# Masked 16-wide cross attention: scores as one float32r pass over four 32-row blocks, transposes two heads behind, values three

## The chip, the cores and the metric

The kernel runs on one core of a Trainium2 chip. The metric is the device time of one execution in microseconds (us), lower is better. TensorE (PE) does the matmuls, VectorE (DVE), ScalarE (ACT) and GpSimd (POOL) the rest; SyncE (SP) issues the DMAs of this stage.

## The reference, cut to what matters

Four layers of cross attention and feed-forward on x of 16 batches x 112 rows x 256, with a context of 16 x 375 x 256. The change touches the first layer's attention alone: 16 heads of width 16, a mask from a running sum, biases.

```
q = (queries @ wq.T + bq).reshape(b, s, h, dh)
k = (patch_representations @ wk.T + bk).reshape(b, p, h, dh)
v = (patch_representations @ wv.T + bv).reshape(b, p, h, dh)
scores = jnp.einsum('bqhd,bkhd->bhqk', q, k) * scale
mask = jnp.arange(p)[None, None, :] > patch_idx[:, :, None]
scores = jnp.where(mask[:, None, :, :], jnp.finfo(scores.dtype).min, scores)
attn = jax.nn.softmax(scores, axis=-1)
out = jnp.einsum('bhqk,bkhd->bqhd', attn, v).reshape(b, s, d)
return out @ wo.T + bo
```

## The kernel before

One function, `cross_attention`, writes three of the four attention stages. With heads of 64 (`wide`) it takes another branch; the first stage is the branch `not wide`. All data are float32. The stage loops over 16 batches and in each over 16 heads, written out as a program for every engine; counters (semaphores) tie them.

For head h TensorE does, in this order: `scores(h)`, a bf16 matmul that adds the mask (identity by `barred`, L451) and a float32 matmul of the head's queries with the keys (L453; the trace has two records for each); `turn(h-1)`, three transposes of the previous head's probabilities (L464); `values(h-2)`, three float32 matmuls (L494, six records). `lag` is the distance of the transposes. The queries lie in `q`, where the 128 rows of a half of the model hold only the head's 16 rows and zeros elsewhere (`headmask`), so the matmul contracts 128 rows of `kT` of which 16 count.

VectorE takes the maximum of a head's scores from PSUM (`head_max`, L752) and copies the transposed probabilities to SBUF (`take_probsT`, L758). ScalarE does the exponential (L608). The scores alternate between two PSUM banks, and the transposes between two.

The projections of the next batch and the output of the last one are cut into pieces, set by hand in the table `order`: behind which head TensorE does K0, K1 (keys, L398), L0, L1 (transposes of the normalised rows), Q0 (queries), V0 to V2 (values), O0 and Y0 (output). They use a ring of two banks, and `slots` says which piece had the bank before. Before the first head of a batch TensorE waits for that batch's Q and K to be taken from PSUM. `first` does the pieces of batch 0 ahead of the heads. SP loads the contexts two batches ahead (L328).

The stages with heads of 64 already split their keys and queries into high and low parts of type float32r (`keys_hi`, `keys_lo`, `q_hh`, `q_ll`) and use three matmuls a head for the scores (L437, L439, L441).

Of the kernel before, what the change touches and what calls it, by code (L numbers as in the profile page):

```python
# [6 lines left out]
F32 = mybir.dt.float32  # L7
# [116 lines left out]
def cross_attention(nc, core, name, ctx_in, w, dh, mask=None):  # L124
# [25 lines left out]
    else:  # L150
        order = {0: ["K0"], 2: ["K1"], 5: ["O0"], 7: ["Y0", "L0", "L1"], 9: ["Q0"], 10: ["V0"],
# [5 lines left out]
    lag = 3 if wide else 1  # L157
    NB = 4 if wide else 2
# [3 lines left out]
    with ctx:  # L162
# [23 lines left out]
        else:  # L186
# [4 lines left out]
            q = [sb(f"q{i}", [P, H, T]) for i in range(2)]  # L191
            kT = [sb(f"kT{i}", [P, EC, S]) for i in range(2)]
# [17 lines left out]
        if mask:  # L210
# [4 lines left out]
            keys = sb("keys", [T, S])  # L215
            headmask = sb("headmask", [P, P // dh])
            barred = [sb(f"barred{i}", [T, S], BF16) for i in range(2)]
# [17 lines left out]
        nweights = 4 + (4 if biased else 0) + (4 if mask else 0)  # L235
# [75 lines left out]
        with nc.Block() as block:  # L311

            @block.sync
            def _(sp):
# [6 lines left out]
                if mask:  # L321
                    sp.dma_start(steps[:, :], mask["steps"]).then_inc(weights.sem, 16)
                    sp.dma_start(upto[:, :], mask["upto"]).then_inc(weights.sem, 16)
                    sp.dma_start(keys[:, :], mask["keys"].partition_broadcast(T)).then_inc(weights.sem, 16)
                    sp.dma_start(headmask[:, :], mask["headmask"]).then_inc(weights.sem, 16)
# [5 lines left out]
                if wide:  # L331
# [13 lines left out]
                    return  # L345
                load(Batch(0, 0))
                load(Batch(0, 1))
                with sp.Fori(0, (B - 2) // 2) as i:
                    for k in (2, 3):
                        b = Batch(i, k)  # L350

                        sp.wait_ge(made["V"].sem, made["V"].at(count("V%d" % (NV - 1), b + -2)))
                        load(b)
# [4 lines left out]
            def _(pe):  # L358
# [67 lines left out]
                def scores(b, h):  # L426
# [29 lines left out]
                def turn(b, h):  # L456
# [4 lines left out]
                    else:  # L461
                        pe.wait_ge(exped.sem, exped.at(H * b.n + h + 1))
                    for j in range(J):
# [20 lines left out]
                def values(b, h):  # L484
# [8 lines left out]
                    for j in range(J):  # L493
                        ins = pe.matmul(bank[0:T, h % G * dh:(h % G + 1) * dh], probsT[h % 2][:, j, :],  # L494
# [3 lines left out]
                def heads(b, b_first, b_last, split_next=True):  # L498
                    where = slots(b_first)
                    for h in range(H):  # L500
# [5 lines left out]
                        if not wide and not (b_first and h < 2):  # L506
# [1952 lines left out]
```

## Time and profile before

| what | value |
|---|---|
| median of three runs | 4162.86 us (4162.65 to 4162.91) |
| time of the profiled execution | 4161.14 us |
| its span, first to last instruction | 4159.3 us |
| TensorE busy | 3536.1 us (85%) |
| VectorE, ScalarE, GpSimd busy | 1574.0, 1536.9, 1197.4 us |
| first score matmul to the last of the stage | 52.6 to 613.7 us |

The time is the span and 1.8 us around it. The masked stage is some 560 of the 4159 us, and the change touches nothing behind it. The profile's slices show TensorE at 9 tenths or more in all of this stage.

### The profile page before, as it was taken

What the parts mean: (1) busy time and instruction counts of PE and PEld (TensorE: products, weight loads), DVE (VectorE), ACT (ScalarE), POOL (GpSimd) and SP (SyncE); (2) the same over time, 40 slices, a digit from 0 to 9 for tenths busy, and PEclk for the clock granted to TensorE, in tenths of its full rate; (3) what the DMA queues carried; (4) which work ended last, traced back from release to release, by engine and by line L of the source; (5) the groups of instructions that cost most, each with busy time, mean ns of one, the idle gap of its engine ahead of it and who ended that gap; (6) DMA issues with size and microseconds to landing.
All of it is one profiled execution on the core that took longest, in us unless ns stands there. A gap on an engine that the chain in (4) does not pass through costs nothing. (4 is left out here: it accounts for less than half of the span.)

```text
span 4159.3 us, 67079 instructions
## 1 busy us (share of the span) xinstructions
PE 3536.1 (85%) x22014; PEld 2897.3 (70%) x22014; DVE 1574.0 (38%) x3464; ACT 1536.9 (37%) x4297; POOL 1197.4 (29%) x1312
## 2 busy tenths in 40 slices
PE   5999992996897873975999999759599999997999
PEld 4777772885565652654889888658488888885665
DVE  3555552001225541014444544300344444444444
ACT  2333330432224550212555555324255444551111
POOL 0000003002000002014666666410466656661000
PEclk9999995998898976987999999779799999997999
DMA  3000002886110003331000000077200000000001
GB/s 117 12 11 11 11 1 82 304 309 211 51 34 4 0 2 106 116 112 34 9 7 9 9 7 5 3 241 280 74 10 9 9 9 9 8 1 12 23 19 33
DMA packets 102019, 240.30 MB, mean 58 GB/s; under 512 B 24682, under 2 KB 73644, under 8 KB 84012
## 3 DMA queue, kind: packets, MB, share of 16 engines
q1 hardware_dynamic: 94188, 219.82, 16.1%
q0 software_dynamic: 7680, 18.36, 1.7%
q8 instruction: 108, 1.77, 0.2%
q14 instruction: 43, 0.35, 0.0%
HBM read 208.78 MB, written 29.36 MB: 57 GB/s over the span
## 5 line engine op out<-in xcount | busy, mean ns | idle before, releaser
L642 POOL TENSOR_SCALAR L_probs<-L_probs,L_inverse 112x375 f32<-112x375 f32 x512 | 645.2, 1260 | 86.9 <-issue 86.9
L752 DVE TENSOR_REDUCE L_negmax<-bank 112x1 f32<-112x375 f32 x768 | 417.5, 544 | 559.7 <-PE bank L441 344.6
L608 ACT ACTIVATE L_probs<-bank,L_negmax 112x375 f32<-112x375 f32 x768 | 439.4, 572 | 407.1 <-DVE L_negmax L752 407.1
L464 PEld LDWEIGHTS bank<-ident,L_probs 112*125 112x125 f32 x2304 | 360.4, 189 | 108.3 <-ACT L_probs L608 47.1
L640 POOL TENSOR_TENSOR L_inverse<-L_sums,neg_one 112x1 f32<-112x1 f32 x512 | 315.2, 616 | 349.7 <-ACT L_probs L608 344.1
L464 PE MATMUL bank<-ident,L_probs 112*125 112x112 f32 x2304 | 376.0, 271 | 22.0 <-issue 10.3
L596 ACT ACTIVATE L_probsT<-bank 125x336 f32<-125x336 f32 x512 | 231.3, 452 | 315.4 <-PE bank L464 313.3
L479 PE MATMUL bank<-L_probsT,v 125*64 125x112 f32 x3072 | 206.1, 270 | 1.1 <-ACT L_probsT L596 1.1
L453 PE MATMUL bank<-L_kT,L_q 128*112 128x375 f32 x512 | 203.5, 478 | 0.0
L437 PE MATMUL bank<-L_keys_hi,L_q_hh 128*112 128x376 f32 x512 | 184.3, 360 | 8.9 <-DVE L_keys_lo L695 6.5
L581 ACT ACTIVATE v<-bank 125x512 f32<-125x512 f32 x192 | 114.9, 598 | 197.3 <-PE bank L391 197.3
L494 PE MATMUL bank<-L_v,L_probsT 125*112 125x16 f32 x1536 | 172.4, 238 | 0.1
L441 PE MATMUL bank<-L_keys_hi,L_q_ll 128*112 128x376 f32 x512 | 171.8, 336 | 0.0
L494 PEld LDWEIGHTS bank<-L_v,L_probsT 125*112 125x112 f32 x1536 | 171.4, 178 | 0.2 <-DVE L_probsT L758 0.2
L439 PE MATMUL bank<-L_keys_lo,L_q_hh 128*112 128x376 f32 x512 | 171.5, 335 | 0.0
L479 PEld LDWEIGHTS bank<-L_probsT,v 125*64 125x64 f32 x3072 | 150.6, 137 | 29.3 <-ACT L_probsT L596 1.6
L1396 ACT ACTIVATE L0t_hidden<-bank,L0t_b 128x128 f32<-128x128 f32 x280 | 102.9, 368 | 170.7 <-PE bank L1356 151.8
L391 PE MATMUL bank<-L_wv_hi,L_ctx_hi 128*125 128x512 f32 x384 | 139.2, 444 | 30.4 <-ACT L_hT L569 30.4
L1356 PE MATMUL bank<-L0t_xT,L0t_w 128*128 128x128 f32 x1120 | 134.8, 279 | 28.3 <-DMA L0t_b<-in_F_b 28.1
L384 PE MATMUL bank<-L_ctx_hi,L_wk_hi 128*128 128x376 f32 x512 | 151.8, 378 | 5.8 <-DVE L_keys_lo L695 5.5
L1356 PEld LDWEIGHTS bank<-L0t_xT,L0t_w 128*128 128x128 f32 x1120 | 131.6, 195 | 36.0 <-issue 35.0
L663 POOL TENSOR_TENSOR L_stats<-L_stats,neg_half 112x1 f32<-112x1 f32 x15 | 8.1, 543 | 507.1 <-DVE L_stats L676 507.1
(272 smaller groups left out, 7070.5 us busy)
## 6 DMA issues: line engine op xcount, KB each, us to landing
L0t_w<-in_F_w SPq DMA_DIRECT2D x70, 1024.0 KB, 5.1
L2t_w<-in_F_w SPq DMA_DIRECT2D x42, 1024.0 KB, 5.2
L_ctxT<-in_ctxT SPq DMA_DIRECT2D x48, 375.0 KB, 3.4
L1t_w<-in_F_w SPq DMA_DIRECT2D x16, 1024.0 KB, 6.2
slots_in<-zeros SPq DMA_DIRECT2D x4, 1792.0 KB, 16.5
L1x_ctxT<-in_ctxT SPq DMA_DIRECT2D x16, 375.0 KB, 3.0
L0t_xs<-slots_in SPq DMA_DIRECT2D x35, 128.0 KB, 6.0
L0t_b<-in_F_b SPq DMA_DIRECT2D x35, 128.0 KB, 6.1
```

The lines of the kernel that those rows point to most:

```text
L437: pe.matmul(psS[h % 2][0:T, 0:SP], q_hh[b.par][:, h, :], keys_hi[b.par][:, c, :], start=True, stop=False)
L441: pe.matmul(psS[h % 2][0:T, 0:SP], q_ll[b.par][:, h, :], keys_hi[b.par][:, c, :], start=False, stop=True).then_inc(scored.sem, 1)
L453: pe.matmul(psS[h % 2][0:T, 0:S], q[b.par][:, h, :], kT[b.par][:, h * dh // P, :], start=False, stop=True).then_inc(scored.sem, 1)
L464: ins = pe.transpose(psT[h % len(psT)][0:SJ, j * T:(j + 1) * T], probs[h % NB][:, j * SJ:(j + 1) * SJ], core.ident[0:T, 0:T])
L479: ins = pe.matmul(bank[i * dh:(i + 1) * dh, at:at + T], v[b.par][0:SJ, j, (h + i) * dh:(h + i + 1) * dh], probsT[(h + i) % NB][:, j, :], s ...
L494: ins = pe.matmul(bank[0:T, h % G * dh:(h % G + 1) * dh], probsT[h % 2][:, j, :], v[b.par][0:SJ, j, h * dh:(h + 1) * dh], start=(j == 0), ...
L596: act.activation(probsT[h % NB][:, :, :], psT[h % len(psT)][0:SJ, 0:J * T].rearrange("p (j t) -> p j t", t=T), ACT.Copy)\
L608: act.activation(probs[h % NB][:, :], psS[h % 2][0:T, 0:S], ACT.Exp, bias=negmax[b.par][:, h:h + 1], accum_out=sums[b.par][:, h:h + 1]).th ...
L640: pool.tensor_tensor(inverse[b.par][:, h:h + 1], sums[b.par][:, h:h + 1], core.neg_one[0:T, :], ALU.pow)
L642: pool.tensor_scalar(probs[h % NB][:, :], probs[h % NB][:, :], inverse[b.par][:, h:h + 1], None, ALU.mult)\
L752: dve.tensor_reduce(negmax[b.par][:, h:h + 1], psS[h % 2][0:T, 0:S], AX, ALU.max, negate=True).then_inc(maxed.sem, 1)
L1356: ins = pe.matmul(psH[f % 4][:, 0:tile], w1[t.par][:, k, f * P:(f + 1) * P], xT[:, k, :], start=(k == 0), stop=(k == DC - 1))
```

## The change

The scores of the masked stage become one float32r matmul. Queries (scaled, with bias) and keys are each split into a high part and the rest (`q_hi`, `q_lo`, `k_hi`, `k_lo`). A pair of heads fills 32 rows; the new tiles `keys4` and `q4` stack four blocks of 32 rows: keys high, low, high, low, and queries high, high, low, low, so one contraction over 128 rows gives all four products. The rows are moved to their blocks by DMA through two buffers in DRAM (`spread_k`, `spread_q`): a batch needs 2 stores and 4 loads for the keys and 2 stores and 8 loads for the queries, all issued by SP in `spread`, with a wait on the stores before the loads. TensorE's wait before the first head of a batch is now for `keys_here` and `q_here`, all of these loads. The transposes run two heads behind, the values three, with four buffers for probabilities and transposed probabilities. The pieces move to other heads. ScalarE writes the high keys, VectorE the low keys and both query parts. Keys and scores have 376 columns, one of them padding. `headmask` is not used here any more, and `q4` is zeroed once at the start.

```diff
-        order = {0: ["K0"], 2: ["K1"], 5: ["O0"], 7: ["Y0", "L0", "L1"], 9: ["Q0"], 10: ["V0"],
+        order = {0: ["K0"], 1: ["K1"], 3: ["L0", "L1"], 4: ["Q0"], 7: ["O0"], 8: ["Y0"], 10: ["V0"],
                  12: ["V1"], 14: ["V2"]}
-    lag = 3 if wide else 1
-    NB = 4 if wide else 2
+    lag = 3 if wide else 2
+    NB = 4
...
+                def spread(b):
+                    sp.wait_ge(taken["K"].sem, taken["K"].at(EC * b.n + EC))
+                    for i, part in enumerate((k_hi, k_lo)):
+                        sp.dma_start(k_dram[i], part[:, :, :].bitcast(F32)).then_inc(k_stored.sem, 16)
+                    sp.wait_ge(k_stored.sem, k_stored.at(32 * b.n + 32))
+                    for quad in range(4):
+                        sp.dma_start(keys4[b.par][32 * quad:32 * quad + 32, :, :].bitcast(F32),
+                                     core.spread_k[quad % 2].rearrange("c (g r) s -> r (c g) s", r=32))\
+                            .then_inc(keys_here.sem, 16)
+
+                    sp.wait_ge(q_split.sem, q_split.at(b.n + 1))
+                    for i, part in enumerate((q_hi, q_lo)):
+                        sp.dma_start(q_dram[i], part[:, :, :].bitcast(F32)).then_inc(q_stored.sem, 16)
+                    sp.wait_ge(q_stored.sem, q_stored.at(32 * b.n + 32))
+                    for quad in range(4):
+                        for e in range(2):
+                            rows = slice(32 * quad + 16 * e, 32 * quad + 16 * e + 16)
+                            sp.dma_start(q4[b.par][rows, e::2, :].bitcast(F32),
+                                         core.spread_q[quad // 2].rearrange("c (g e r) t -> e r (c g) t", e=2, r=16)[e])\
+                                .then_inc(q_here.sem, 16)
...
-                        pe.wait_ge(taken["Q"].sem, taken["Q"].at(NQ * b.n + NQ))
-                        pe.wait_ge(taken["K"].sem, taken["K"].at(EC * b.n + EC))
+                        pe.wait_ge(q_here.sem, q_here.at(128 * b.n + 128))
+                        pe.wait_ge(keys_here.sem, keys_here.at(64 * b.n + 64))
...
-                    pe.matmul(psS[h % 2][0:T, 0:S], core.ident_b[0:T, 0:T], barred[b.par][:, :],
+                    pe.wait_ge(exped.sem, exped.at(H * b.n + h - 1))
+                    pe.matmul(psS[h % 2][0:T, 0:SP], core.ident_b[0:T, 0:T], barred[b.par][:, :],
                               start=True, stop=False)
-                    pe.matmul(psS[h % 2][0:T, 0:S], q[b.par][:, h, :], kT[b.par][:, h * dh // P, :],
+                    pe.matmul(psS[h % 2][0:T, 0:SP], q4[b.par][:, h, :], keys4[b.par][:, h // 2, :],
                               start=False, stop=True).then_inc(scored.sem, 1)
...
-                        if not wide and not (b_first and h < 2):
-                            values(*before(b, h, 2))
+                        if not wide and not (b_first and h < 3):
+                            values(*before(b, h, 3))
...
+                        act.activation(k_hi[:, m, 0:S], bank[:, 0:S], ACT.Identity, bias=bk[:, m:m + 1])\
+                            .then_inc(k_high.sem, 1)
...
+                    if p[0] == "K" and not wide:
+                        dve.wait_ge(k_high.sem, k_high.at(EC * b.n + m + 1))
+                        dve.scalar_tensor_tensor(out=k_lo[:, m, 0:S], in0=bank[:, 0:S], scalar=bk[:, m:m + 1],
+                                                 in1=k_hi[:, m, 0:S].bitcast(F32), op0=ALU.add, op1=ALU.subtract)\
+                            .then_inc(taken["K"].sem, 1)
...
-                            ins = dve.scalar_tensor_tensor(
-                                out=q[b.par][:, c * HC:(c + 1) * HC, :],
-                                in0=bank[:, c * T:(c + 1) * T].unsqueeze(1).broadcast_to([P, HC, T]),
-                                scalar=bq[:, c:c + 1], in1=headmask[:, :].unsqueeze(2).broadcast_to([P, HC, T]),
-                                op0=ALU.add, op1=ALU.mult)
+                            ins = dve.tensor_scalar(qs[:, c, :], bank[:, c * T:(c + 1) * T], bq[:, c:c + 1], scale,
+                                                    ALU.add, ALU.mult)
+                        ins.then_inc(taken["Q"].sem, 1)
+                        dve.drain()
+                        dve.tensor_copy(q_hi[:, :, :], qs[:, :, :])
+                        dve.drain()
+                        dve.tensor_tensor(q_lo[:, :, :], qs[:, :, :], q_hi[:, :, :].bitcast(F32), ALU.subtract)\
+                            .then_inc(q_split.sem, 1)
```

TensorE before, heads 2 and 3 of a batch in the loop, with piece K1 behind head 2 (L451 and L453 are the scores, L464 the transposes, L494 the values):

```order
L451 MATMUL bank0<-L0_barred1,ident_b 112x375
L453 MATMUL bank0<-L0_kT1,L0_q1 112x375
L462 REGISTER_ALU
L464 MATMUL bank3<-ident,L0_probs1 125x112 x3
L488 REGISTER_ALU
L491 REGISTER_ALU
L494 MATMUL bank5<-L0_v1,L0_probsT0 112x16 x3
L398 MATMUL bank7<-L0_ctxT0,L0_wk 128x375 x2
L451 MATMUL bank1<-L0_barred1,ident_b 112x375
L453 MATMUL bank1<-L0_kT1,L0_q1 112x375
```

Behind head 2's scores stand the transposes of head 1 and the values of head 0.

TensorE after the change, heads 3 and 4 with the pieces L0, L1 and Q0 (the same operations are L488, L490, L502 and L532 now, L405 and L412 the pieces):

```order
L488 MATMUL bank1<-L0_barred1,ident_b 112x376
L490 MATMUL bank1<-L0_keys41,L0_q41 112x376
L502 MATMUL bank3<-ident,L0_probs1 125x112 x3
L529 REGISTER_ALU
L532 MATMUL bank5<-L0_v1,L0_probsT0 112x16 x3
L400 ISA
L404 REGISTER_ALU
L405 MATMUL bank6<-ident,L0_normed 128x112
L400 REGISTER_ALU
L405 MATMUL bank7<-ident,L0_normed 128x112
```

With head 3's scores stand the transposes of head 1 and the values of head 0; Q0 follows one head behind L1, where it stood two behind.

VectorE after the change, head 4 and the start of head 5 (L800 is the maximum, L806 the copy of transposed probabilities, L827 and L830 the division of the last batch, L764 to L770 the queries' scaling and split):

```order
L800 TENSOR_REDUCE L0_negmax1<-bank0 112x1
L806 COPY L0_probsT2<-bank2 125x336
L827 RECIPROCAL L0_inverse<-L0_sums0 112x16
L830 TENSOR_TENSOR L0_o<-bank4,L0_inverse 112x256
L764 TENSOR_SCALAR L0_qs<-bank6,L0_bq 128x112 x2
L768 CAST L0_q_hi<-L0_qs 128x224
L770 TENSOR_TENSOR L0_q_lo<-L0_qs,L0_q_hi 128x224
L799 REGISTER_ALU
L800 TENSOR_REDUCE L0_negmax1<-bank1 112x1
```

Before, the division stood at head 3 and the queries' two operations at head 9; now both stand between the maxima of heads 4 and 5.

SP in the loop, after the change (L359 to L373 is `spread` of one batch, L335 the load of a context):

```order
L359 DMA spread_k<-L0_k_hi 128x2x376
L359 DMA spread_k<-L0_k_lo 128x2x376
L360 ISA
L362 DMA L0_keys40<-spread_k 32x8x376 x4
L366 REGISTER_ALU
L368 DMA spread_q<-L0_q_hi 128x2x112
L368 DMA spread_q<-L0_q_lo 128x2x112
L373 DMA L0_q40<-spread_q 16x8x112 x8
L378 ISA
L335 ISA
L335 DMA L0_ctxT0<-in_ctxT 128x750
```

Before, only the last of these rows, the context's load, stood there.

## Rows read from the trace of the kernel before

**Rows 1.** By stretch: length, busy PE, PEld, DVE, ACT, POOL; clock, DMA share, GB/s.

```profile
42.40:52.40 10.00, 9.45 (x30) 6.39 (x31) 2.46 (x3) 2.34 (x6) 0.00 (x0) 1.00 0.00 0
52.40:613.70 561.30, 554.64 (x3620) 438.09 (x3618) 312.18 (x659) 217.70 (x646) 8.15 (x15) 1.00 0.03 10
```

**Rows 2.** Groups of instructions by line, 52 to 613 us.

```profile
L752 DVE TENSOR_REDUCE L_negmax<-bank 112x1 f32<-112x375 f32 x255 | 139.7, 548 | 213.1 <-PE bank L453 212.6
L758 DVE COPY L_probsT<-bank 125x336 f32<-125x336 f32 x254 | 126.4, 498 | 1.7
...
L720 DVE SCALAR_TENSOR_TENSOR L_q<-bank,L_bq,L_headmask 128x896 f32<-128x896 f32 x30 | 33.1, 1146 | 12.6 <-PE bank L376 12.6
```

**Rows 3.** Timeline of one head, a key piece, the next head (start, duration).

```profile
304.63 0.35 PE L451 MATMUL bank<-L_barred,ident_b 112*112 112x375 bf16 x1
...
304.82 0.80 PE L453 MATMUL bank<-L_kT,L_q 128*112 128x375 f32 x2
...
305.45 0.48 PE L464 MATMUL bank<-ident,L_probs 112*125 112x112 f32 x3
...
305.74 0.55 DVE L752 TENSOR_REDUCE L_negmax<-bank 112x1 f32<-112x375 f32 x1
305.76 0.67 PE L494 MATMUL bank<-L_v,L_probsT 125*112 125x16 f32 x6
...
306.20 0.50 DVE L758 COPY L_probsT<-bank 125x336 f32<-125x336 f32 x1
...
306.29 1.51 PE L398 MATMUL bank<-L_ctxT,L_wk 128*128 128x375 f32 x4
306.32 0.57 ACT L608 ACTIVATE L_probs<-bank,L_negmax 112x375 f32<-112x375 f32 x1 [1.08 <-DVE L_negmax L752]
...
307.63 0.32 PE L451 MATMUL bank<-L_barred,ident_b 112*112 112x375 bf16 x1
```

**Rows 4.** TensorE's timeline in the second attention: a float32r score matmul and the next.

```profile
2106.01 0.33 PE L441 MATMUL bank<-L_keys_hi,L_q_ll 128*112 128x376 f32 x1
2106.18 0.48 PE L464 MATMUL bank<-ident,L_probs 112*125 112x112 f32 x3
```

**Rows 5.** Timeline of the start: key pieces, first scores.

```profile
45.38 4.74 PE L398 MATMUL bank<-L_ctxT,L_wk 128*128 128x375 f32 x8
...
52.61 0.32 PE L451 MATMUL bank<-L_barred,ident_b 112*112 112x375 bf16 x1
```

**Rows 6.** DMA issues of the page: count, KB of each, median us to landing.

```profile
L0t_w<-in_F_w SPq DMA_DIRECT2D x70, 1024.0 KB, 5.1
...
L_ctxT<-in_ctxT SPq DMA_DIRECT2D x48, 375.0 KB, 3.4
...
slots_out<-L1t_ys SPq DMA_DIRECT2D x8, 448.0 KB, 3.4
...
L3d_wg<-in_F_wg SPq DMA_DIRECT2D x18, 128.0 KB, 2.0
...
out<-x SPq DMA_DIRECT2D x1, 1792.0 KB, 7.9
```

**Rows 7.** SP's time for one issue: to a padded tile (L333), to a contiguous one.

```profile
L333 SPq DMA_DIRECT2D L_ctxT<-in_ctxT x32: 540/549/671, 1894.4 to 3609.7; - x32
...
L328 SPq DMA_DIRECT2D L_ctxT<-in_ctxT x16: 332/333/615, 32.4 to 513.8; - x16
```

**Rows 8.** Busy time by stretch around a pause of TensorE, second attention.

```profile
1948.00:1952.00 4.00, 2.26 (x7) 1.79 (x8) 0.84 (x2) 1.12 (x5) 3.14 (x4) 0.82 0.00 0
1952.00:1956.00 4.00, 4.00 (x20) 3.52 (x19) 0.79 (x2) 2.21 (x5) 1.17 (x2) 0.75 0.00 0
```

**Rows 9.** Groups of instructions by line, VectorE, splits in the later attentions.

```profile
L695 DVE SCALAR_TENSOR_TENSOR L_keys_lo<-bank,L_bk,L_keys_hi 128x376 fp32r<-128x376 f32 x128 | 77.8, 608 | 178.0 <-ACT L_keys_hi L571 177.3
...
L730 DVE CAST L_ctx_hi<-L_ctxT 128x752 fp32r<-128x752 f32 x32 | 20.4, 638 | 6.8 <-DMA L_ctxT<-in_ctxT 6.6
```

**Rows 10.** Timeline of the start: GpSimd clears a tile (start, duration).

```profile
4.54 3.52 POOL L93 MEMSET zeros<- 112x4096 f32 x1
```

More of the change, by code:

```diff
@@ L214, in cross_attention @@
             last_key = sb("last_key", [T, B])
-            keys = sb("keys", [T, S])
-            headmask = sb("headmask", [P, P // dh])
-            barred = [sb(f"barred{i}", [T, S], BF16) for i in range(2)]
+            keys = sb("keys", [T, SP])
+            barred = [sb(f"barred{i}", [T, SP], BF16) for i in range(2)]
             barred_ready = core.counter("barred_ready")
@@ L323, in _ @@
                     sp.dma_start(upto[:, :], mask["upto"]).then_inc(weights.sem, 16)
-                    sp.dma_start(keys[:, :], mask["keys"].partition_broadcast(T)).then_inc(weights.sem, 16)
-                    sp.dma_start(headmask[:, :], mask["headmask"]).then_inc(weights.sem, 16)
+                    sp.dma_start(keys[:, 0:S], mask["keys"].partition_broadcast(T)).then_inc(weights.sem, 16)
                 def load(b):
@@ L345, in _, with next_load @@
                     return
+                k_dram = [core.spread_k[i].rearrange("c p s -> p c s") for i in range(2)]
+                q_dram = [core.spread_q[i].rearrange("c p t -> p c t") for i in range(2)]
+                def spread(b):
[17 more added lines that the diff above has]
+                                .then_inc(q_here.sem, 16)
+                def next_load(b):
+                    sp.wait_ge(made["V"].sem, made["V"].at(count("V%d" % (NV - 1), b + -2)))
+                    load(b)
                 load(Batch(0, 0))
@@ L348, in _ @@
                 with sp.Fori(0, (B - 2) // 2) as i:
[L349 to L353, printed above, removed]
+                    spread(Batch(i, 0))
+                    next_load(Batch(i, 2))
+                    spread(Batch(i, 1))
+                    next_load(Batch(i, 3))
+                spread(Batch(0, B - 2))
+                spread(Batch(0, B - 1))
                 sp.wait_ge(core.zeroed_sem, 16 * (core.slots_in.shape[0] // (B * T)))
@@ L493, in values @@
                     for j in range(J):
-                        ins = pe.matmul(bank[0:T, h % G * dh:(h % G + 1) * dh], probsT[h % 2][:, j, :],
+                        ins = pe.matmul(bank[0:T, h % G * dh:(h % G + 1) * dh], probsT[h % NB][:, j, :],
                                         v[b.par][0:SJ, j, h * dh:(h + 1) * dh], start=(j == 0), stop=(j == J - 1))
@@ L528, in tail @@
                     else:
+                        turn(b, H - 2)
+                        values(b, H - 3)
                         turn(b, H - 1)
@@ L832, in tail @@
                     if not wide:
-                        take_probsT(b, H - 1)
+                        for h in range(H - lag, H):
+                            take_probsT(b, h)
                     divide(b, NG - 1)
@@ L852, in _ @@
                 if mask:
+                    dve.memset(keys[:, S:SP], 0.0)
+                    for part in (k_hi, k_lo):
+                        dve.memset(part[:, :, S:SP].bitcast(F32), 0.0)
+                    for part in q4:
+                        dve.memset(part[:, :, :].bitcast(F32), 0.0)
                     dve.tensor_copy(stepsf[:, :], steps[:, :]).then_inc(setup_done.sem, 1)
@@ L870, in cross_attention @@
                 s.stage_over(16 * B // 2)
+            k_high.stage_over(B * EC)
+            q_split.stage_over(B)
+            for s in (k_stored, q_stored):
+                s.stage_over(32 * B)
+            keys_here.stage_over(64 * B)
+            q_here.stage_over(128 * B)
         for s in (var_ready, rstd_ready, normed_ready):
@@ L2313, in STAGES @@
     l3 = {n: a["L3_" + n] for n in ("wq", "wk", "wv", "wo", "bq", "bk", "bv", "bo")}
-    m = {n: a[n] for n in ("steps", "upto", "keys", "headmask")}
+    m = {n: a[n] for n in ("steps", "upto", "keys")}
     f0 = {n: a["F0_" + n] for n in ("wg", "w1", "b1", "w2", "b2")}
```

41 lines of the change are left out of this document (25 added, 16 removed).

## The prediction

> **What bounds the kernel now.** I read the profile in this order: the slices of the page, the busy time by stretch, the groups by line in the masked stage, one head's timeline, and then rows of later stages for operations that this stage does not have yet. In the stretch of all heads TensorE is busy 554.6 of 561.3 us, VectorE 312, ScalarE 218 [rows 1]: TensorE sets the pace, and its queue has work from head to head. The timeline of one head shows what it spends: 0.19 us from the mask's matmul to the scores', 0.63 from there to the transposes, 0.31 to the values, 0.53 to the next work, 1.66 us in all [rows 3]. The starts follow each other without a gap, so each difference is the price of the operation before it. 256 heads at 1.66 are 425 us; what is left of 561 us, some 138 us, are the pieces of 15 batches, 9.2 us each. A full batch so takes 16 x 1.66 + 9.2 = 35.8 us.
>
> **The score matmul.** It goes from one float32 matmul to one float32r matmul of the same size. A float32r matmul of 376 columns is followed by the next work after 0.17 us in the second attention [rows 4]. So 0.63 becomes 0.17: 0.46 us a head. From the first scores to the last there are 255 heads: -117 us. Bounds: that row has the same 128 rows and 112 columns of weights, so I see no reason for more than 0.20; -109 is the weak end. The mask's matmul keeps its 0.19. A plain head then needs 1.20 us and a batch 16 x 1.20 + 9.2 = 28.4 us of TensorE.
>
> **What VectorE can't hide any more.** In a head it does a maximum and a copy, 0.55 and 0.50 us [rows 2], starting 0.46 apart [rows 3], so about 1.0 of the 1.20 us. It has 0.2 us a head to spare where it had 0.6. With the lags of two and three the chain is loose in a plain head: the scores are made 0.5 us after the head's start, the maximum ends at 1.1, the exponential (0.57 [rows 3] and the reading of its sum) at about 1.9, and its bank is wanted again at 2.4; the copy of the transposes of a head ends 0.3 us before its values are wanted. Anything long between two maxima eats that 0.3. The long blocks: low parts of the keys, 0.61 us each [rows 9], which also wait for ScalarE's high part; behind them the normalising, 0.4; and at head 4 the queries. Those were two operations of 1.15 us, 2.3 in all [rows 2], at head 9, when a head took 1.66. Now they are four: two scalings of 112 columns at about 0.25, a cast of 224 columns below the 0.64 of 752 columns, a subtraction of 224 below the 0.61 of 376 [rows 9]; I take 1.5 us with the drains, and the division (0.7) stands just ahead. Following the queues through a batch I get TensorE waiting 0.5 us at the values of head 3's step (the copy comes late behind both low keys), 0.25 before Q0 (one head behind L1, not two), 0.75 at head 6's step behind the query split, and 0.25 before Y0 (one head behind O0): 1.75 us a batch, 15 times, +26 us. Bounds: 0.5 and 3 us a batch (+8, +45); the lower if pieces of TensorE cover the blocks, the upper if each block lands whole on TensorE.
>
> **The spreading by DMA.** None of this is in the trace, and it is the large unknown. Its path: K1 is made 4.9 us into a batch (two heads and two key pieces, 2 x 1.20 + 2 x 1.25 to 1.34 [rows 3]), ScalarE's high part takes 0.57 and the low part 0.61, so SP wakes at about 6.3 us. An issue to a padded tile costs SP 0.55 us, to a contiguous one 0.33 [rows 7]; here all 16 are of the first kind. Two stores of 376 KB: a store of 448 KB lands after 3.4 us and one of 1792 KB after 7.9, so 3.35 us per MB [rows 6]; 3.4 + 1.2 for the second and its issue make 4.9. Four loads of 376 KB: 375 KB land after 3.4, 1024 KB after 5.1 [rows 6], 2.6 us per MB; 3.4 + 2.9 = 6.3 for the last. The two stores of queries (112 KB each) are issued meanwhile and land behind them, 0.7 later. Eight small loads are 8 x 0.55 of SP and 2.0 until the last has landed, as 128 KB take [rows 6]: 6.5. In sum 4.9 + 7.0 + 6.5 = 18.4 us, ready at 24.7 us into the batch, where TensorE wants the next batch's scores at 28.4 + 1.75 = 30.15. It is hidden with 5.4 us to spare, and then costs nothing; if that cover is gone, each us beyond costs 15 us.
>
> A load that writes only 32 partitions has no row here: the rows of 375 KB and 1024 KB write 128 [rows 6]. The Trainium skill, SBUF — State Buffer, in the section on the port swizzle of the DMA door, states that 32 partitions reach only half of the ports and so get half of the bandwidth. By that rule the key loads would take 5.2 us per MB, 9.3 us in place of 6.3, and the set is ready at 27.7 us, still ahead of 30.15; only the start would lose 3 us more, and the sum would be 4099 in place of 4096.
>
> **The start.** Batch 0 has nothing to hide the spreading behind. VectorE first clears the two `q4`, 1792 columns each; GpSimd clears 4096 columns in 3.52 us [rows 10], so 3.1 us for both by that rate, ahead of all the rest. The key pieces ended at 45.38 + 4.74 = 50.1 [rows 5]; with 3.0 for clearing, 1.2 for both key parts and 18.4 for the DMAs the first scores start at 72.8, not at 52.6 [rows 5]: +20. TensorE pauses in between. A pause has a second price: in the second attention, where TensorE was busy 2.26 of 4 us, the granted clock was 0.82 in that stretch and 0.75 in the next though it was busy all the time [rows 8], so half clock for a part of each. At the start eight records of K took 4.74 us, where four later take 1.34, from 306.29 to 307.63 [rows 3]: almost twice as long each. Some 8 us of work at half clock cost 4 us. Start in all: +24 us (bounds +15, if clearing costs little and the DMAs are quick, and +30).
>
> **Other edits, at nothing.** Moving the pieces costs only the waits above. The stage's end has one more pair of transposes and values behind the last head, under 1 us. The loads of the next context stand behind the spreading on SP, and have most of a batch before their keys are due. 376 columns in place of 375 is a quarter of a per cent of a matmul. All other stages are the same.
>
> **Sum.** -117 + 26 + 24 = -67 us against the profiled execution's 4161.1 us: 4094. The median of the runs is 1.7 us above that execution, so 4096 for the median.
>
> **Rivals.**
> 1. *The queues absorb the blocks* and the start is cheap: 0.5 us a batch and +15: -117 + 8 + 15 = -94, 4069. For it: TensorE's pieces often stand where VectorE is late. Against it: 0.2 us of spare time a head.
> 2. *The spreading ends after TensorE.* It takes 26 us in place of 18.4: ready at 32.3, 2.15 us late, 15 times, +32, and 8 at the start: 4136. For it: four DMA round trips in a row, rows of 448 bytes in the query loads, none seen here. With the clock falling at each boundary, as in [rows 8], another 1 to 2 us a batch: 4151 to 4166.
> 3. *Slower than before*, the same mechanism beyond its turning point. The batch period becomes 6.3 + chain. The gain left by the sum is 67 us plus the 5.4 us of cover of 15 batches; 16 x (chain - 18.4) has to exceed 67 + 81, so the chain must take over 27.7 us, or some 26 with the half clock on top. At 30 us: period 36.3, 15 x 6.15 + 12 more than the sum: 4200. For it: SP's issue of a three-level pattern may be dearer than 0.55, and small runs slower. Against it: every row has landed in 2.0 to 3.4 us for its size.
> 4. *VectorE becomes the bound* in every head: 1.35 us a head by it rather than 1.20 gives back 38 us: 4134.
>
> **How the numbers follow.** My sum 0.55, rival 1 0.13, rival 2 0.15, rival 3 0.12, rival 4 0.05. About 0.2% (8 us) is what a measurement of this kernel can tell from no change. Faster by more: 0.85; within: 0.03, the upper part of rival 2; slower: 0.12. The likeliest case's own range is 4075 to 4115; the range that takes in rival 4, most of rival 2 and half of rival 1 is 4066 to 4150.
>
> **What the profile would show.** Right: score matmuls of float32r 0.17 us before the transposes; a plain head of about 1.2 us; a batch of about 30 us; first scores near 73 us; TensorE waiting for VectorE's copies near heads 3 and 6, and never for a DMA at a batch's first head except batch 0. The last score matmul at about 545 us. Wrong: TensorE waiting for `q4` or `keys4` each batch, SP's waits for stores longer than 5 us, or a granted clock below 1.0 inside the stage.

## The result, and the profile after

The changed kernel takes 4049.55 us (median of 4 executions, 4045.55 to 4061.3), the one before 4162.75 (4156.43 to 4162.91): ratio 0.9736, 95% interval 0.9714 to 0.9758, so 113 us less. Forecast were 4096 and a range of 4066 to 4150. The direction was right, and the time lies 16 us below the range.

The profiled execution has a span of 4048.0 us, 111.3 less than before. Between landmarks that both programs have (the first load of a stage's weights, the first and last score matmul) it splits like this:

| stretch | before | after | difference |
|---|---|---|---|
| start to first score matmul | 52.6 | 72.9 | +20.3 |
| first to last score matmul | 560.5 | 463.9 | -96.6 |
| second attention, its code untouched | 815.4 | 814.3 | -1.1 |
| fourth attention, its code untouched | 849.5 | 819.1 | **-30.4** |
| all the rest | 1881.3 | 1877.8 | -3.5 |

The masked stage gave 76 us, 9 more than the 67 of the sum. The 30 us of the fourth attention were no part of any case.

Busy time by stretch after, in the columns of [rows 1]: the pause of batch 0 and the stage.

```profile
52.90:72.90 20.00, 2.99 (x12) 1.96 (x12) 0.61 (x1) 1.59 (x4) 0.00 (x0) 0.70 0.67 153
72.90:537.00 464.10, 450.15 (x3353) 406.19 (x3353) 308.90 (x718) 215.31 (x644) 8.12 (x15) 0.97 0.46 109
```

TensorE still sets the pace, busy 450 of 464 us where it was 555 of 561. VectorE works as long as before, 309 us, and so is at two thirds where it was at 56%. New is a clock under 1.00.

A head in the timeline after, against [rows 3] (start, duration):

```profile
301.43 0.35 PE L488 MATMUL bank<-L_barred,ident_b 112*112 112x376 bf16 x1
301.48 0.47 PE L490 MATMUL bank<-L_keys,L_q 128*112 128x376 f32 x1
301.79 0.48 PE L502 MATMUL bank<-ident,L_probs 112*125 112x112 f32 x3
302.10 0.67 PE L532 MATMUL bank<-L_v,L_probsT 125*112 125x16 f32 x6
```

From the mask's matmul to the transposes it is now 0.36 us, where 0.19 and 0.63 stood. The two starts overlap, so only their sum says something: 0.46 us less, as in [rows 4]. A duration misleads here: the score matmul lasts 0.47 and its successor starts 0.31 behind it.

What TensorE and the others wait for, 72.9 to 537 us (total, times, longest):

```profile
POOL L_stats L702 <- DVE L_stats L715: 437.0, 15, 34.8
ACT L_probs L647 <- DVE L_negmax L800: 220.9, 255, 18.0
DVE L_negmax L800 <- PE bank L490: 107.3, 149, 19.9
...
PE bank L488 <- DMA L_q<-spread_q: 16.9, 1, 16.9
...
PE bank L532 <- DVE L_probsT L806: 13.9, 30, 0.9
```

VectorE's idle time before a maximum fell from 213 us [rows 2] to 107. TensorE has two short waits a batch for the copied probabilities, and one long one for a DMA, in batch 0. The two in one batch, values of head 3's step and of head 6's:

```profile
315.46 0.76 PE L532 MATMUL bank<-L_v,L_probsT 125*112 125x16 f32 x6 [0.33 <-DVE L_probsT L806]
...
320.97 0.76 PE L532 MATMUL bank<-L_v,L_probsT 125*112 125x16 f32 x6 [0.53 <-DVE L_probsT L806]
```

The spreading on SP's queue from one batch to the next, which the trace before did not have:

```profile
285.60 0.38 SPq L359 DMA_DIRECT2D spread_k<-L_k_hi  x1
286.02 0.47 SPq L359 DMA_DIRECT2D spread_k<-L_k_lo  x1
289.17 1.80 SPq L362 DMA_DIRECT2D L_keys<-spread_k  x4
291.17 0.38 SPq L368 DMA_DIRECT2D spread_q<-L_q_hi  x1
291.59 0.48 SPq L368 DMA_DIRECT2D spread_q<-L_q_lo  x1
299.07 3.63 SPq L373 DMA_DIRECT2D L_q<-spread_q  x8
307.23 0.37 SPq L335 DMA_DIRECT2D L_ctxT<-in_ctxT  x1
314.56 0.38 SPq L359 DMA_DIRECT2D spread_k<-L_k_hi  x1
```

The batch's period is 314.56 - 285.60 = 28.96 us. The eight issues of the query loads end at 302.7; the last of them starts at 302.3 and lands 2.2 later, at 304.4: a chain of 18.8 us. Median us to landing, to be read beside [rows 6]:

```profile
L_keys<-spread_k SPq DMA_DIRECT2D x64, 376.0 KB, 6.0
...
L_q<-spread_q SPq DMA_DIRECT2D x128, 56.0 KB, 2.2
spread_k<-L_k_hi SPq DMA_DIRECT2D x16, 376.0 KB, 2.5
```

**The fourth attention.** The DMA queues over that stage show what differs in code that nobody edited. Before, 2951 to 3760 us (packets, MB, share), and TensorE's timeline of a piece of it:

```profile
q8 instruction: 63, 1.03, 0.6%
```

```profile
3125.10 0.51 PE L384 MATMUL bank<-L_ctx_hi,L_wk_lo 128*128 128x376 f32 x2
3127.97 0.51 PE L437 MATMUL bank<-L_keys_hi,L_q_hh 128*112 128x376 f32 x1 [2.37 <-issue]
3128.28 0.52 PE L439 MATMUL bank<-L_keys_lo,L_q_hh 128*112 128x376 f32 x1
3128.60 0.52 PE L441 MATMUL bank<-L_keys_hi,L_q_ll 128*112 128x376 f32 x1
3128.91 0.39 PE L464 MATMUL bank<-ident,L_probs 112*125 112x112 f32 x1
3130.62 0.55 PE L464 MATMUL bank<-ident,L_probs 112*125 112x112 f32 x2 [1.32 <-issue]
```

After, 2870 to 3650 us:

```profile
q8 instruction: 17, 0.28, 0.1%
```

The queue of instruction fetches brings 63 packets of 16 KB where it brings 17 after. The stage's loop has six turns of two batches each. After, no packet comes between 3030 and 3517 us, in turns two to six. Before, nine packets come in each of these turns, 45 of the 46 more: the loop's code, and more, once again each time. TensorE then stands on "issue" (it waits for nothing that the profile shows), and behind the pause its matmuls run at half clock. The branches at the ends of TensorE's turns give the price of a turn. The last three rows are of runs described below:

| loop | packets in the stage | turns two to six, us |
|---|---|---|
| fourth attention, before | 63 | 100.6, 101.4, 99.9, 99.6, 100.9 |
| fourth attention, after | 17 | 94.2 each |
| second attention, after | 18 | 91.3 each |
| second attention, `twohops` | 27 | 95.2, then 91.3 each |
| second attention, `qsplit` | 36 | 95.2, 95.4, then 91.3 each |
| second attention, `fill` | 63 | 99.0, 97.2, 98.4, 98.8, 98.6 |

A turn that is fetched again takes nine packets and 4 to 8 us more. Busy time of 100 us, before and then after:

```profile
3200.00:3300.00 100.00, 93.41 (x685) 84.18 (x684) 44.24 (x87) 49.87 (x127) 60.53 (x65) 0.97 0.03 9
```

```profile
3200.00:3300.00 100.00, 97.83 (x743) 88.38 (x740) 46.38 (x92) 52.88 (x136) 65.21 (x71) 1.00 0.03 8
```

TensorE's busy share goes from 93.4 to 97.8, its clock from 0.97 to 1.00, in a loop whose own code is the same.

### The profile page after: what moved, and what is told of

Its sections match the earlier page's. It is cut to its first block and busy times, and to the rows that moved or that the text cites. A ratio compares the mean times of both kernels' runs of the same rounds, so it can differ in the third digit from the quotient of the medians.

```text
span 4048.0 us, 67301 instructions
## 1 busy us (share of the span) xinstructions
PE 3418.4 (84%) x21758; PEld 2856.8 (71%) x21758; DVE 1574.2 (39%) x3533; ACT 1533.1 (38%) x4297; POOL 1196.3 (30%) x1312
## 5 line engine op out<-in xcount | busy, mean ns | idle before, releaser
L800 DVE TENSOR_REDUCE L_negmax<-bank 112x1 f32<-112x375 f32 x768 | 417.2, 544 | 445.4 <-PE bank L477 335.9
L502 PE MATMUL bank<-ident,L_probs 112*125 112x112 f32 x2304 | 374.6, 271 | 9.5 <-POOL L_probs L681 8.3
L502 PEld LDWEIGHTS bank<-ident,L_probs 112*125 112x125 f32 x2304 | 363.0, 190 | 17.6 <-POOL L_probs L681 15.3
L532 PE MATMUL bank<-L_v,L_probsT 125*112 125x16 f32 x1536 | 178.7, 242 | 14.0 <-DVE L_probsT L806 13.9
L532 PEld LDWEIGHTS bank<-L_v,L_probsT 125*112 125x112 f32 x1536 | 175.3, 181 | 19.4 <-DVE L_probsT L806 15.9
L1631 ACT ACTIVATE L3d_silu<-bank 128x448 f32<-128x448 f32 x72 | 39.1, 543 | 301.7 <-PE bank L1595 301.7
L647 ACT ACTIVATION_READ_ACCUMULATOR L_probs<-bank,L_negmax 112x1 f32 x768 | 150.5, 196 | 0.0
```

The costliest lines, as they stand in the source:

```text
L502: ins = pe.transpose(psT[h % len(psT)][0:SJ, j * T:(j + 1) * T], probs[h % NB][:, j * SJ:(j + 1) * SJ], core.ident[0:T, 0:T])
L647: act.activation(probs[h % NB][:, :], psS[h % 2][0:T, 0:S], ACT.Exp, bias=negmax[b.par][:, h:h + 1], accum_out=sums[b.par][:, h:h + 1]).th ...
L800: dve.tensor_reduce(negmax[b.par][:, h:h + 1], psS[h % 2][0:T, 0:S], AX, ALU.max, negate=True).then_inc(maxed.sem, 1)
```

## The experiments

The theory: two thirds of the gain come from the cheaper score matmul, and the rest from the position of the fourth attention's loop in TensorE's program, which the edit of the masked stage moved. Rivals: the new lags and the order bring the gain; the fourth attention is faster for something that the stage left in memory or in the clock.

**1 and 2. Moving code without changing work** (`after_pad`, `before_pad`). A wait that has long been satisfied is added 170 times to the changed kernel, which gives TensorE the 85 instructions that it has less of ahead of the loop than before (two waits make one instruction), and 342 times, 171 instructions, to the kernel before.

```diff
+                if name == "L0":
+                    for _ in range(170):
+                        pe.wait_ge(core.filled_sem, 1)
                 pe.wait_ge(weights.sem, weights.at(16 * len(loads)))
```

> The changed kernel, with 85 instructions more on TensorE (satisfied waits) at the start of the first routing stage, where TensorE waits for its loads anyway, so that all its later code lies as far along as in the kernel before. Theory A, the 30 us gained in the fourth attention come from where TensorE's loop lies in instruction memory: the fetches of instructions come back (before had 63 blocks in that stage, the changed kernel 17), TensorE pauses about 2.3 us twice in each of six turns of its loop, and that stage takes about 849 us in place of 819; the whole is about 30 us over the changed kernel, 4075 to 4085. Rival B, the 30 us are chance or come from the clock or from data: the stage stays at 819 and the whole within 8 us of 4050.

> The kernel before, with 171 instructions more on TensorE at the same place, which brings the code of the fourth attention to the same place within a block of 256 instructions as in the changed kernel. Theory A: no refetching there, the stage takes about 819 us, the whole 4125 to 4140. Rival B: still 849 us, the whole within 8 us of 4163. If the place that counts is not the one within 256 instructions, A can hold and this run stay at 849.

The padded changed kernel: 4072.9 us (4072.41 to 4083.05, 4 executions), ratio to before 0.9811, interval 0.9788 to 0.9834; its fourth attention takes 849.6 us, with these packets from 2870 to 3650:

```profile
q8 instruction: 62, 1.02, 0.6%
```

The padded kernel before: 4129.72 us (7 executions, before 4155.01), ratio 0.9945, interval 0.9928 to 0.9962; its fourth attention takes 818.2 us, and from 3200 on it looks like after:

```profile
3200.00:3300.00 100.00, 97.83 (x749) 88.61 (x750) 48.00 (x95) 53.42 (x137) 64.58 (x71) 1.00 0.04 12
```

So 31 us can be switched on and off in either kernel by waits that cost nothing. The rival of something left behind falls. The totals moved by less, 23 us up (4072.9, just under the 4075 to 4085 expected) and 25 down: in the one profiled execution the masked stage was 4.5 us shorter than in that of after, in the other the second attention took 821.3 us with 27 packets in place of 815.4 with 18.

**3. New lags and order, old scores** (`fp32_pipe`). The kernel before, with transposes two behind, values three, four buffers, and the new table; the scores stay one float32 matmul.

```diff
-    lag = 3 if wide else 1
-    NB = 4 if wide else 2
+    lag = 3 if wide else 2
+    NB = 4
...
```

> The kernel before with the new lags (transposes two behind, values three), four buffers, the new table of pieces and the new waits, but scores still one float32 matmul of 128 masked rows. If TensorE's own work was the bound, the masked stage gets at most the wait of the normalised rows' transposes back (0.35 us a batch): first to last score matmul 552 to 562 us, from 560.7. Rival, the lags carry part of the gain: under 545 us. The fourth attention may come out at either 819 or 849 us, since the code moves.

First to last score matmul 555.5 us in place of 560.5, clock 1.00 throughout, 15 waits for the copies with 6.1 us in all. Order and lags by themselves are worth 5 us; they are the cover for the cheaper matmul and no gain of their own. (In all 4117.83 us, but 33 of that is again the fourth attention, 816.7 us.)

**4. The old lags with the new scores** (`lag1`): transposes one head behind, values two.

```diff
-    lag = 3 if wide else 2
+    lag = 3 if wide else 1
...
-                        if not wide and not (b_first and h < 3):
-                            values(*before(b, h, 3))
+                        if not wide and not (b_first and h < 2):
+                            values(*before(b, h, 2))
...
```

> The changed kernel with the transposes one head behind the scores and the values two, as before. The transposes of head h-1 need its exponential, done about 1.9 us after that head's start, and TensorE asks for it 1.55 us after it: some 0.35 us of waiting in each head without a piece. Eleven or so heads of sixteen: about 4 to 6 us a batch, first score to last about 530 to 560 us in place of 464. Rival, the lag is not needed: 464 to 475.

Measured: 629.1 us for the stage and 4218.42 in all, slower than before (4155.01) and far outside what I expected. The waits of TensorE on ScalarE's probabilities are only 23.0 us in 29 places. The size is in the clock, here in four stretches of 40 us:

```profile
113.00:153.00 40.00, 38.46 (x184) 34.72 (x185) 17.95 (x41) 11.83 (x37) 0.20 (x1) 0.59 0.37 85
153.00:193.00 40.00, 37.99 (x246) 31.20 (x244) 22.19 (x50) 15.63 (x45) 0.88 (x2) 0.90 0.37 85
193.00:233.00 40.00, 38.92 (x189) 34.57 (x189) 18.95 (x43) 12.15 (x37) 0.06 (x1) 0.62 0.36 85
233.00:273.00 40.00, 38.70 (x213) 34.14 (x212) 19.97 (x43) 13.89 (x41) 0.48 (x1) 0.70 0.36 85
```

TensorE is busy 95 to 97% of these stretches and slow: 1.5 us of waits a batch come with a clock that costs some 140 us more than in after (629.1 less 463.9 and the 23 of waits). The lags are a condition of the change.

**5. The old table with the new scores** (`oldorder`).

```diff
-        order = {0: ["K0"], 1: ["K1"], 3: ["L0", "L1"], 4: ["Q0"], 7: ["O0"], 8: ["Y0"], 10: ["V0"],
+        order = {0: ["K0"], 2: ["K1"], 5: ["O0"], 7: ["Y0", "L0", "L1"], 9: ["Q0"], 10: ["V0"],
```

> The changed kernel with the pieces at their heads of before (K1 behind head 2, O0 5, Y0, L0, L1 7, Q0 9). The queries are then split about 9 us later, near 21 to 22 us into a batch; their stores (some 3.5 us, nothing is ahead of them on the DMA queues any more) and eight loads (5.8 us) end near 31 us, 2 us after the next batch's scores are wanted at 28.9. Theory: TensorE waits for the query loads 1 to 3 us in each batch, and its clock falls behind some of these waits: first to last score 490 to 560 us in place of 464. Rival, there is cover enough: 460 to 475, no wait for the loads.

477.6 us for the stage, below the 490 to 560 expected, and 4082.26 in all. The queries are stored only at 300 us and land in their blocks at 308, nearly when they are wanted: TensorE waits four times for them, 20.1 us, 17.0 of it in batch 0. The new table is worth some 14 us here, not the whole change. Behind batch 0 some 4 us of these are waits (18.1 us against 13.9, with 5.3 of them again for L0); most of the rest goes with a half clock that here holds from 517 us to the stage's end.

**6. A longer chain** (`twohops`): the keys are copied twice more inside DRAM before they are loaded.

```diff
+                    for hop in range(2):
+                        for i in range(2):
+                            sp.dma_start(core.hop_k[hop][i].rearrange("c p s -> p c s"),
+                                         (core.spread_k if hop == 0 else core.hop_k[0])[i].rearrange("c p s -> p c s"))\
+                                .then_inc(hopped.sem, 16)
+                        sp.wait_ge(hopped.sem, hopped.at(64 * b.n + 32 * hop + 32))
...
```

> The changed kernel with the keys copied twice more, from DRAM to DRAM (752 KB each), before they are loaded: each copy about 4 to 6 us. The DMA chain takes 27 to 31 us in place of 18.9, SP starts it 6.5 us into the batch. By the rule of the prediction (batch period = 6.5 + chain where that is more than TensorE's own 28.9) the period is 34 to 37 us, TensorE waits 5 to 8 us a batch, with the clock at half behind each wait another 1 to 3: first to last score 560 to 610 us, so about as slow as the kernel before. Rival, DMAs of two batches overlap and the period stays near 29.

TensorE's waits over the stage:

```profile
PE bank L495 <- DMA L_q<-spread_q: 125.1, 16, 26.8
PE bank L539 <- DVE L_probsT L813: 11.5, 23, 1.1
```

Now it waits for the DMA in every batch, the stage takes 622.3 us, and the whole 4226.01 us (before: 4153.07), both above what I expected. This is rival 3 of the prediction, brought about by a longer chain, and half of its rule holds. The chain from the first key store to the last query load's landing is 28.1 to 29.9 us, 28.8 in the mean, and the period, 39.2 in the mean, follows it. But what stands ahead of the chain is not 6.3 us. It is 9.2 to 11.6 us from the third batch on, 10.4 in the mean, with TensorE at half clock behind each wait: four records of keys take 2.85 us at 319 us, where they take 1.51 in after. By the ends of the stage (613 us before, 706 here, and 537 where the chain is hidden, which it is up to 28.96 - 6.5 = 22.5 us) the turning point lies at about 25 us of chain on a straight line, an estimate, where the prediction had 26 to 27.7. The change itself has 22.5 - 18.8, some 3.6 us, to spare.

**7. VectorE's long block taken apart** (`qsplit`, `qsplit_again`): the division stands behind head 3 in place of 4, the queries' high part behind head 5, the low one behind 6, the mask behind 8.

```diff
+                            if h == 5:
+                                high_query()
+                            if h == 6:
+                                low_query()
...
```

> The changed kernel with VectorE's long block behind head 4 taken apart: the division stands behind head 3's maximum, the high part of the queries behind head 5's, the low part behind head 6's, the mask of the next batch behind head 8's. TensorE's 0.53 us of waiting at the values there should go, and the 0.33 us at head 3's may grow by the division: batch period 28.2 to 28.9 us from 28.93, with the clock at full through more of the stage: first to last 445 to 462 us. Rival, the waits only move: 460 to 466.

> The kernel with the query split spread over heads 3 to 8 once more, unchanged. Its first trace had the first attention in 445.6 us at full clock after its start, and the second attention in 823.8 us with 36 instruction packets where after has 18. If this second refetch belongs to the placement of the code: again 822 to 826 us and 36 packets. If it is a matter of the single execution: some other pair. If shorter waits of TensorE are what keeps the clock up in the first attention: again 445 to 448 us and 1.00 from 100 to 500 us.

445.6 and 445.4 us for the stage against 463.9 of after: 8 us fewer in waits (5.9, one wait a batch), and the rest of the 18 goes with the clock, which here stays up once it has risen. The second execution:

```profile
73.00:77.00 4.00, 3.42 (x8) 2.15 (x8) 1.22 (x4) 0.68 (x3) 0.56 (x1) 0.50 0.35 96
77.00:81.00 4.00, 4.00 (x16) 2.86 (x15) 1.62 (x4) 1.80 (x4) 0.00 (x0) 0.70 0.00 0
81.00:519.00 438.00, 430.63 (x3330) 391.77 (x3330) 302.12 (x712) 211.02 (x638) 7.56 (x14) 1.00 0.49 115
```

The totals differ, 4037.86 and 4023.67 us: the second attention took 823.8 us with 36 instruction packets in the one and 814.3 with 18 in the other, from one and the same program.

**8. The start** (`start`): the first batch's queries stored and loaded ahead of its keys, and the `q4` cleared before the wait for the weights.

```diff
+                def spread_first(b):
+                    sp.wait_ge(q_split.sem, q_split.at(b.n + 1))
...
-                    for part in q4:
-                        dve.memset(part[:, :, :].bitcast(F32), 0.0)
...
```

> The changed kernel with two edits of its start: VectorE clears the two query tiles while it waits for the weights (3.8 us less ahead of the first pieces), and for batch 0 alone SP stores and loads the queries ahead of the keys, which are made later (4 to 6 us less, since the query stores no longer queue behind the key loads). First scores at 62 to 66 us in place of 72.9, the rest as it was. Rival, TensorE's pause just stays: first scores later than 69.

First scores at 66.6 us in place of 72.9 (62 to 66 expected), last at 526.0. In all 4050.93 us, no better than after, since the second attention took 827.1 (36 packets again).

**9. The changed kernel once more** (`after_again`).

> The changed kernel once more, unchanged. If the loops whose code is fetched again are decided by where the code lies, this run repeats the trace of after: fourth attention 817 to 821 us, second 813 to 816, 63 packets on the instruction queue. If it is a matter of the single execution, one of these three numbers moves (second attention towards 824 to 827, or fourth towards 849). First to last score matmul: 460 to 466 us if the two stretches of half clock in the first attention stand at the same places again, 449 to 455 if the later one is an accident.

4053.27 us; fourth attention 816.2, second 814.2, 63 packets in the program. The half clock came near the start again, and longer, from 85 to 115 us; the later stretch, at 467 to 481 us in after, was absent. First to last 466.1: neither of the two cases expected, since the place and the length both changed in one and the same program.

**10. Work in the pause** (`fill`): 70 matmuls of the identity, which nobody reads, before TensorE's wait in batch 0.

```diff
+                            for _ in range(70):
+                                pe.matmul(psT[0][:, 0:P], core.ident[:, :], core.ident[:, :], start=True, stop=True)
```

> After, with 70 matmuls of the identity by itself (128 columns, fp32, into a bank that is free then) in TensorE's pause before the first score matmul; nothing reads their result. If the clock at a stretch's start follows from the engine having stood idle before it, the first 4 us after the first score matmul at 73 us show 1.00 in place of half, and first to last score matmul falls from 463.9 by 2 to 6 us. If only the later work decides, nothing moves. Rival: the pile of matmuls outlasts the wait and the first score matmul comes later than 74 us.

The stretches of the pause, of the first heads, and of what follows:

```profile
56.00:73.00 17.00, 17.00 (x147) 16.72 (x145) 0.00 (x0) 0.77 (x2) 0.00 (x0) 1.00 0.72 166
73.00:77.00 4.00, 1.89 (x9) 1.25 (x9) 1.09 (x4) 0.66 (x2) 0.00 (x0) 1.00 0.58 144
...
81.00:85.00 4.00, 3.58 (x29) 3.58 (x29) 2.54 (x7) 2.28 (x8) 0.00 (x0) 0.88 0.56 197
85.00:89.00 4.00, 4.00 (x21) 3.99 (x21) 3.17 (x9) 1.22 (x4) 0.00 (x0) 0.50 0.90 210
```

The heads begin at full clock, as the first theory has it, and first to last is 458.0 us, 5.9 shorter. The first score matmul comes at 75.2, though, later than the 74 of the rival (and than 72.9; 74.8 in `after_again`, without the filling). But the clock falls later all the same, at 84 us. And the 70 matmuls moved the code: now the *second* attention is the one fetched again, 63 packets and 851.2 us in place of 18 and 814.3, and the kernel takes 4073.03 us. TensorE's longest wait there is 5.5 us on "issue". It is the same effect in another loop, 37 us here, brought about by a third edit ahead of it.

**11. Three edits together** (`combo`): 7, 8, and 40 of the matmuls of 10.

> After with three edits together: the first batch's queries are stored and loaded ahead of its keys and the clearing of the query buffers comes before the wait for the weights (first score matmul at 66 to 67 us), the query split spread over heads 3 to 8 (first to last score matmul 445 to 455 us), and 40 matmuls of the identity in TensorE's pause. Stage end at 522 to 533 us, 14 to 25 us ahead of after's 546.9. With the other stages as in after: 4025 to 4036 us. If the second attention's loop is fetched again as in the two kernels that this one is made of (10 to 13 us): 4035 to 4049. If the placement moved by the 40 matmuls makes the fourth attention's loop a fetched one: 30 us more, 4055 to 4079, slower than after.

4028.42 us (4026.37 to 4034.51, 5 executions), ratio to before 0.9697, interval 0.9683 to 0.971, just clear of the change's own 0.9714 to 0.9758, and 16 us less by the ratios. First score matmul at 67.7, last at 512.4, clock 1.00 from 74 us on; both loops are at their short times, 814.5 and 818.5 us.

## Why the prediction was right in direction and wrong in size

**The score matmul, -117: right.** 0.46 us a head as [rows 4] had it, and experiment 3 shows that the matmul carries the gain.

**VectorE, +26: two of the four places right, the size twice too large.** The waits at the values of head 3's step and at head 6's came, 0.33 and 0.53 us where I had 0.5 and 0.75; those before Q0 and Y0 did not. 0.86 us a batch are 13 us. My prices for the queries' work were near, as the groups of VectorE's instructions show:

```profile
L764 DVE TENSOR_SCALAR L_qs<-bank,L_bq 128x112 f32<-128x112 f32 x30 | 8.6, 329 | 3.4 <-PE bank L412 3.4
...
L770 DVE TENSOR_TENSOR L_q_lo<-L_qs,L_q_hi 128x224 fp32r<-128x224 f32 x15 | 5.9, 392 | 1.1
...
L768 DVE CAST L_q_hi<-L_qs 128x224 fp32r<-128x224 f32 x15 | 4.2, 277 | 1.4
```

Over 15 batches 18.7 us, so 1.25 us a batch, and 0.17 of idle time between them, for my 1.5. So it was not the blocks' length that I had wrong: following the queues gave two waits that never came and made the other two too long.

**A wait that went away, -5: missing.** Before, L0's transposes stood behind Y0 and waited for VectorE, 5.2 us in 14 places; the new table parts them.

**The start, +20 ahead of the first scores: right.** They come at 72.9, forecast 72.8. The two clearings, against [rows 10]:

```profile
39.84 1.55 DVE L906 MEMSET L_q<- 128x1792 f32 x1 [0.32 <-issue]
41.72 1.55 DVE L906 MEMSET L_q<- 128x1792 f32 x1 [0.32 <-issue]
```

1.55 us each, forecast 3.1 for both.

**The spreading, hidden: right.** A chain of 18.4 forecast, 18.8 measured, against a period of 28.96; it costs in batch 0 alone. The parts were off in both directions. The key stores took 3.6 us (285.60 to 289.17) for my 4.9. The key loads with the queries' stores behind them took 9.9 (289.17 to 299.07) for 7.0. The query loads took 5.4 for 6.5.

The rule of the Trainium skill, SBUF — State Buffer, on the port swizzle, made the key loads 9.3 in place of 6.3, so 10.0 in place of 7.0 for this middle part. The trace agrees with it: 9.9 for the middle part, and the four key loads by themselves take 9.2, from 289.17 to the last one's landing at 298.4; a single one lands after 6.0 us in the median and 8.4 at most. The rows of 128 partitions were too hopeful a measure, and in the loop the 3 us are hidden by either.

**The clock, 4 us at the start: too small.** It cost about 13, as what is left of the stage: -96.6 + 118 for the matmul (255 heads at 0.463) - 13 for the waits + 5. That fits 29 us of the stage at half clock, 5 of them up to 78 us. After the start there were two stretches at half clock, 1.2 GHz, 88 to 99 and 467 to 481 us, where before had 1.00 in the whole stage; the prediction had named a clock below 1.0 as a sign of being wrong. (It had also taken the 4.74 us of the first key pieces for half clock, where the column has 1.00 [rows 1]; why those records are so long stays open.) Each follows on one of the two short waits:

```profile
85.00:89.00 4.00, 3.47 (x28) 3.29 (x28) 3.51 (x9) 1.99 (x6) 0.00 (x0) 0.91 1.05 229
89.00:93.00 4.00, 4.00 (x23) 4.00 (x21) 2.11 (x4) 1.33 (x4) 0.00 (x0) 0.50 1.01 198
```

TensorE paused 0.53 us at 86 us, and its granted clock fell to half behind that, while it was busy all the time. But the same wait stands in the other 13 batches and no fall followed, so a wait is at most what allows it. Experiments 4 and 7 show that more waiting goes with more half clock and less with none behind the start; what decides in a single case stays open.

**The step that failed: "All other stages are the same."** This is where the range broke. The sum's stage was 9 us pessimistic, and that by errors that cancel in part: 13 too much for VectorE's waits and the missing 5 one way, 9 too little for the clock the other. Without the 30 us of the fourth attention the time would have been 4080, well inside the range; they brought it to 4050. The term stood in the sum at nothing, for the one reason that no line of those stages is edited. Experiments 1 and 2 show that the position of its loop in TensorE's code makes them, and 10 that the second attention has the same trap. The profile of before had it in view: 108 instruction packets in the program, and pauses of 2.3 us on "issue" in a loop of pure matmuls. I read only the stage that the edit touched.

Which positions are bad is not shown, only made likely. The Trainium skill, Advanced Engine Details and Errata, ISA Cache, gives TensorE 128 KB in lines of 16 KB, 256 instructions. The 16 KB are those of a packet. Its "Only 2 cache lines!" is not borne out here: the traces have 1580 and 1564 instructions of TensorE in a turn of the fourth and second attention, 6.2 and 6.1 such lines, and these loops can run turn after turn without a packet (after, 3030 to 3517 us). The 171 instructions of `before_pad` are 256 less 85, so it has the loop where after has it within a line, and it came out like after; `after_pad` has it where before has it, and came out like before.

By my count in the compiled programs the loops fetched again each turn ended 0.94 (`fill`) and 0.98 (before, `after_pad`) into a line, those that were not, at 0.75 or less. The second attention ended at about 0.85 in nine profiled executions, and of these four had 18 packets, two 27 and three 36: none, one or two turns fetched again, always the second, or the second and third. No trace shows these places as such; the distances from kernel to kernel come out the same, to 0.02 of a line, when TensorE's instructions in the traces are counted. A fetch that runs ahead past the loop's end, and drives out its beginning, would bring the nine packets for a loop that lies in seven lines. That is argued, and no run tried positions one by one.

## What to carry to other kernels

- With loops as long as these (1580 instructions, 101 KB of code by the count above), an edit anywhere ahead of a loop can move its time by about 4%. Compare the instruction queue's packets of each stage before believing a gain, or pad with satisfied waits to tell it apart from the edit's own.
- When the bounding engine gets cheaper by a quarter, price the next engine's long blocks, and break them up between its short deadlines: here it gave 8 us in waits, and the other 10 of its 18 us came with a clock that stayed up.
- A chain of DMAs off the path costs nothing until it reaches the period, and then all of it, and the half clock behind each wait on top: know the slack in us, here 3.6.

## What the runs showed of the hardware that was not expected

- One and the same program can fetch a loop's code again in one execution and not in the next (`qsplit`: 36 and 18 packets, 823.8 and 814.3 us), and then for its second and third turn alone.
- A loop of six turns whose code is fetched again in each costs TensorE 30 to 37 us on top of 814 to 819: pauses of about 2.3 us, and up to 5.5, and half clock behind them.
- With TensorE 96% busy the granted clock of a stretch of 40 us was as low as 0.59 (`lag1`), with 29 waits of under 1.2 us in the whole stage.
